# Macaron block on eight cores: an integer weight load moved to another queue, a wait on its stash added, and the second LayerNorm taken in another order

## The chip, the cores and the metric

The kernel runs on one Trainium2 chip, on 8 cores. Each core computes one of the eight batch entries (2048 tokens by 1024 features) with the same program; no core waits for another. The metric is device time in microseconds of the slowest core.

## The reference, cut to what matters

The block is: half a feed-forward step, an attention step, half a feed-forward step, each with a LayerNorm ahead and a residual.

```
def ffn(x):                      # k0 [2048,4096], k1 [4096,4096], k2 [4096,1024], booleans
    W = lambda k: where(k, 1.0, -1.0)
    h = concatenate([x, -x], -1)
    h = relu(s0 * h @ W(k0)) * 2
    h = relu(s1 * h @ W(k1)) * 2
    return s2 * h @ W(k2)

def attn(x):                     # causal linear attention, 16 heads of 64, buckets of 64
    q = softmax(scale * x @ Wq.T per head);  k = elu(scale * x @ Wk.T) + 1;  v = x @ Wv.T
    context = cumsum over buckets of k^T v, divided by (cumsum of sum k + eps), shifted by a bucket
    return (q @ context) @ Wo.T + bo

x = x + 0.5 * ffn(layernorm(x))
x = x + attn(layernorm(x))
x = x + 0.5 * ffn(layernorm(x))
```

Since the input of the first layer is [x, -x], the kernel uses one weight matrix of half the height for it: W(k0[:1024]) - W(k0[1024:]), which is 2 * (k0 upper - k0 lower).

## The kernel before, in words

There is no scheduler. The program appends instructions to five streams (one an engine) in the order in which Python calls `b.op` and `b.dma` (lines 64 to 107), and each instruction carries the semaphore waits of what it reads. A DMA stands in the stream of the engine that issues it, and an engine runs its stream in order: a DMA on ScalarE is issued only after every activation ahead of it. The DMAs of SP, ScalarE (ACT) and GpSimd (POOL) rotate over eight semaphores each (qs, qa, qg), and a DMA also waits for the one eight before it on its own rotation (line 101).

**First feed-forward** (`ffn_phase`). The tokens are taken in two halves of 1024. The first LayerNorm half fills `xnf`. Then `l0_half` (line 402) makes layer 0: eight blocks `nb` of 512 hidden features. In the first half of the first feed-forward only (`build and half == 0`, lines 409 to 430) each block's weights are made from the integers:

- `ta`, a DMA on SP, loads the upper half of k0's block (128 x 8 x 512 bytes, 512 KB) into `u8a`; `tb`, a DMA on ScalarE, loads the lower half into `u8b`. Both wait for the subtraction of the block before, which frees the two buffers.
- L418, VectorE: the subtraction into `wst[:, nb % 2]`; it waits for both loads, for the matmuls of block nb-2 and for the stash of block nb-2 (two weight slots alternate).
- L424, VectorE: the product with the scale, in place.
- `st_["t_w_stash"]`, a DMA on SP: the finished block (1 MB, bf16) is written to `d0_scr` in DRAM, from where later halves read it.
- L446, TensorE: 64 matmuls of 128x128 by 128x512 (4 groups of features by 2 of tokens by 8 deep), which wait for `tslot`, the product. L457, ScalarE: eight Relu evictions into `a1`.

Meanwhile POOL has issued four casting DMAs that turn the attention weights from float32 to bf16 in DRAM (`wprep`, `wbf_scr`); nothing gates them, so they start at the program's start. Layer 1 (L512) and layer 2 (L572) follow, with weight blocks that POOL loads into four slots. During layer 2 of the second half, `ln2_hook` (line 995) computes the statistics of the attention's LayerNorm. For the 128-token chunks gc 0 to 7 it loads them from DRAM, one after the other, into the two pages of `xst` (page gc % 2), so that chunks 6 and 7 are what stands in `xst` at its end. For chunks 8 to 15 it reads them where layer 2 leaves them.

**Attention** (`attn_phase`, line 599). After a fence of all engines and queues, all 16 chunks are loaded from `x_scr`: 0 to 7 by ScalarE's queue into the space of `qfm`, 8 to 15 by POOL's into the space of `kk`; SP issues 16 DMA transposes for Wq and Wk. For each chunk in turn L297 (VectorE) normalizes into `qb`, eight transposes on TensorE (L310) fill `ps_t`, and L317 (VectorE) copies them to `xn2fm`. `ps_t` and the order in VectorE's stream make it a chain, chunk after chunk. Then the projections (L700) run for q, k and v over 16 chunks each.

Of the kernel before, what the change touches and what calls it, by code (L numbers as in the profile page):

```python
# [162 lines left out]
def build_program(debug_phases=("ffn1", "attn", "ffn2")):  # L163
    b = B()
# [13 lines left out]
    x_dram = nc.dram_tensor("x_scr", [T, D], F32, kind="Internal").ap()  # L178
# [11 lines left out]
    xst = b.sb("xst", [128, 2, D], F32)  # L190
    qb = b.sb("qb", [128, 2, D], BF16)
# [14 lines left out]
    def t7_set(i, tok):  # L206
# [5 lines left out]
    st_ = {  # L212
        "pa": [None, None, None],
        "pb": [None, None, None, None],
        "pt": None,
        "xst": [None, None],
        "qb": [None, None, None],
        "qfm_gate": None,
        "scr1": None, "scr2": None,
        "mv": [None, None],  # L220
# [38 lines left out]
    def ln_load(src_ap, gc, page, pg_tok, q):  # L259
        return b.dma(q, page, chunk_ap(src_ap, gc),  # L260
                     reads=(pg_tok, st_["x_load_extra"][gc]))
# [60 lines left out]
    def ffn_phase(src_ap, dst_ap, fstack, l2_hook=None):  # L322
# [5 lines left out]
        u8b = b.sb(None, [128, 8, 512], U8, fstack)  # L328
# [72 lines left out]
        def l0_half(half, t_xn_last):  # L401
            rp = 0
            nonlocal a1_evac
            for nb in range(8):
                sl = nb % 2
                dsl = wst[:, sl, 0:8, :]
                d0blk = d0_dram[:, nb * 512:(nb + 1) * 512].rearrange(
                    "(cc p) n -> p cc n", p=128)
                if build and half == 0:
                    ta = b.dma("sync", u8a[:],  # L410
                               k0_d[0:D, nb * 512:(nb + 1) * 512]
                               .rearrange("(cc p) n -> p cc n", p=128),
                               reads=(u8_tok[0],))
                    tb = b.dma("scalar", u8b[:],
                               k0_d[D:2 * D, nb * 512:(nb + 1) * 512]
                               .rearrange("(cc p) n -> p cc n", p=128),
                               reads=(u8_tok[1],))
                    td1 = b.op("vector", lambda E, ds=dsl: E.tensor_tensor(  # L418
                        out=ds, in0=u8a[:], in1=u8b[:], op=ALU.subtract),
                        (ta, tb, st_["wstq"][sl], st_["slot_stash"][sl], t_d0c),  # L420
                        "dv")
                    u8_tok[0] = td1
                    u8_tok[1] = td1
                    tslot = b.op("vector", lambda E, ds=dsl: E.tensor_scalar(  # L424
                        out=ds, in0=ds, scalar1=deriv[:, 0:1], scalar2=None,
                        op0=ALU.mult), (), "dv")
                    st_["t_w_stash"] = b.dma("sync", d0blk, dsl,
                                             reads=(tslot,))
                    st_["slot_stash"][sl] = st_["t_w_stash"]
                    tslot = (tslot,)  # L430
                else:
                    tslot = b.dma("sync", dsl, d0blk,
                                  reads=(st_["wstq"][sl], st_["slot_stash"][sl],
                                         st_["t_w_stash"]))
                    tslot = (tslot,)
                grp_last = None
                for n in range(4):
                    for th in range(2):
                        rp = st_["rot7"]
                        st_["rot7"] = (rp + 1) % 7  # L440
                        reads = tslot + (t_xn_last[th * 4 + 3], t7_tok(rp))
                        mm = None
                        for cch in range(8):
                            mm = b.op("tensor",
                                      lambda E, r=rp, nn=n, t2=th, c3=cch, ds=dsl:
                                      E.matmul(tile7[r],  # L446
                                               ds[:, c3, nn * 128:(nn + 1) * 128],
                                               xnf[:, c3, t2 * 512:(t2 + 1) * 512],
                                               start=(c3 == 0), stop=(c3 == 7)),
                                      reads if cch == 0 else (),  # L450
                                      "pe" if cch == 7 else None)
                        grp_last = mm
                        ev_reads = [mm]
                        if nb == 0 and n == 0 and th == 0:
                            ev_reads.append(st_["prev_xh_store"])
                        tev = b.op("scalar", lambda E, r=rp, nn=n, t2=th, nb2=nb:
                                   E.activation(out=a1[:, nb2 * 4 + nn,  # L457
                                                       t2 * 512:(t2 + 1) * 512],
                                                in_=tile7[r], func=AF.Relu),
                                   ev_reads, "ac")  # L460
                        t7_set(rp, tev)
                        a1_evac = tev
                st_["wstq"][sl] = grp_last
            l0_pe[half] = grp_last
# [134 lines left out]
    def attn_phase(astack):  # L599
# [23 lines left out]
        def ln2_page(gc):  # L623
            if gc < 8:
                return qfmx[:, gc, :]
            j = gc - 8
            return kkxs[:, 2 * j:2 * j + 2, :, :].rearrange(
                "p a b c -> p (a b c)")

        ln2_tx = [ln_load(x_dram, gc, ln2_page(gc), st_["ln2_stage_gate"],  # L630
                          "scalar" if gc < 8 else "gpsimd")
                  for gc in range(16)]
        stage_tok = [None] * 16
        xn2_tok = [None] * 16
        twt_cur = None
        soft_pe = ("pe", b.cnt["pe"], "_")
        for gc in range(16):
            if gc == 8:
                twt_cur = load_wT(wTsA, 0, (t_wstash["q"],))
            mv, trs = st_["ln2_pre"][gc]  # L640
            sl = gc % 2
            txn, _ = ln_apply(sl, gc, mv, trs, ln2_tx[gc], ln2_page(gc),
                              False, lambda s: qb[:, s, :], (st_["qb"][sl],))
            stage_tok[gc] = txn
            st_["qb"][sl] = txn
            t_xn_last = transpose8(
                lambda c3, s=sl: qb[:, s, c3 * 128:(c3 + 1) * 128],
                xn2fm[:, :, gc * 128:(gc + 1) * 128], (txn, soft_pe))
            st_["qb"][sl] = t_xn_last
            xn2_tok[gc] = t_xn_last  # L650
# [29 lines left out]
        for wname in ("q", "k", "v"):  # L680
# [7 lines left out]
                                    ("pe", b.cnt["pe"], "_")))  # L688
            else:
                wTs, twt = wTsA, twt_next  # L690
            for tc in range(16):
                rb = tc % 3
                mm = None
                for jb in range(2):
                    for c in range(8):
# [10 lines left out]
                if wname == "q":  # L706
# [7 lines left out]
                        axis=AX.X), (t4,), "dv")  # L714
                    b.op("vector", lambda E: E.reciprocal(
                        out=stat[:, 5, :], in_=stat[:, 5, :]), (), "dv")
                    sl = tc % 3
                    t7 = b.op("vector", lambda E, s=sl: E.tensor_tensor(
                        out=qpage(s).rearrange("p (h e) -> p h e", e=64),
                        in0=scr1[:, :].rearrange("p (h e) -> p h e", e=64),  # L720
# [6 lines left out]
                elif wname == "k":  # L727
                    while st_["q_pend"]:
                        q_flush()
                    sl = tc % 2  # L730
                    tmx = b.op("vector", lambda E, r=rb, s=sl: E.tensor_scalar(
                        out=qb[:, s, :], in0=qps[r][:, :], scalar1=SCALE_Q,
                        scalar2=0.0, op0=ALU.mult, op1=ALU.max),
                        (mm, st_["qb"][sl]), "dv")
                    te = b.op("scalar", lambda E, r=rb: E.activation(  # L735
                        out=scr1[:], in_=qps[r][:, :], func=AF.Exp,
                        scale=SCALE_Q), (tmx, st_["scr1"]), "ac")
                    qps_tok[rb] = te
                    t4_reads = (te, tmx, stage_tok[8 + tc // 2])
                    if tc == 15:  # L740
                        t4_reads = t4_reads + (st_["qb"][2],)
                    t4 = b.op("vector", lambda E, t2=tc, s=sl: E.scalar_tensor_tensor(
                        out=kk[:, t2, :, :].rearrange("p h e -> p (h e)"),
                        in0=scr1[:], scalar=1.0, in1=qb[:, s, :],
                        op0=ALU.min, op1=ALU.add), t4_reads, "dv")
                    st_["scr1"] = t4
                    st_["qb"][sl] = t4
                    kk_tok[tc] = t4
                else:
                    tv = b.op("vector", lambda E, t2=tc, r=rb: E.tensor_copy(  # L750
                        out=vv[:, t2, :, 0:128], in_=qps[r][:, :]
                        .rearrange("p (h e) -> p h e", e=128)), (mm,), "dv")
                    qps_tok[rb] = tv
                    vv_tok[tc] = tv
# [332 lines left out]
```

How the kernel before makes its waits and increments, by code:

```python
                def body(E):  # L131
                    seen = {}
                    nw = 0
                    for item in self.streams[eng]:
                        if item[0] == "w":
                            _, s, v = item
                            if seen.get(s, 0) >= v:
                                continue
                            seen[s] = v
                            if nw >= 2:
                                E.nop(nofuse=True)
                                nw = 0
                            E.wait_ge(self.semh[s], v)
                            nw += 1
                        else:
                            nw = 0
                            _, fn, inc, amt = item
                            inst = fn(E)
                            if inc is not None and amt:
                                inst.then_inc(self.semh[inc], amt)
```

## Time and profile before

| what | us |
|---|---|
| median of 2 timed runs (3943.73 to 3957.61) | 3950.67 |
| the profiled execution, its own time | 3531.66 |
| its span, core 3, the slowest | 3530.1 |
| spans of the eight cores | 3495.0 to 3530.1 |
| mean granted TensorE clock of the cores | 0.938 to 0.946 |
| TensorE busy with matmuls, core 3 | 3073.8 |

The profiled execution is one run of the same program; the two timed runs took 419 us longer, and the traces hold nothing of them. All rows below are of core 3 in the profiled execution, and their times count from its first instruction.

### The profile page before, as it was taken

How to read it: one execution, taken by the hardware profiler on the slowest of the kernel's cores; microseconds unless marked ns; L12 is line 12 of the kernel's file. 1: busy time of each engine (PE TensorE's matmuls, PEld its weight loads, DVE VectorE, ACT ScalarE, POOL GpSimd, SP SyncE). 2: the span in 40 equal slices, each digit the busy share in tenths (PEclk: the TensorE clock that was granted, in tenths of full speed). 3: DMA queues.
4: the chain of work that ended last, by engine and by line, in shares of the span. 5: the costliest groups of instructions: out<-in, count | busy, mean ns of one | idle time of the engine just before them, and what ended most of it. 6: DMA issues, size and time to landing. Idle time of an engine off the chain costs nothing.

```text
span 3530.1 us, 35801 instructions; the slowest of 8 cores (3495.0 to 3530.1 us)
## 1 busy us (share of the span) xinstructions
PE 3073.8 (87%) x14600; PEld 1404.2 (40%) x14600; DVE 532.5 (15%) x593; ACT 444.5 (13%) x745; POOL 168.7 (5%) x208
## 2 busy tenths in 40 slices
PE   0558999988999999984886678999999989999998
PEld 0223444443444444432433423444444444444443
DVE  2122111111000000023655831000000000000001
ACT  0111101000120110000112402210110021011000
POOL 0000000000000000000000000000000000000000
PEclk9878999999999999996996588999999999999999
DMA  9225546455232231437101072332233222221322
GB/s 146 78 78 152 171 126 175 135 162 174 84 96 72 71 96 60 133 112 168 22 14 30 12 232 58 91 100 78 84 90 105 84 85 91 75 84 60 96 96 96
DMA packets 223409, 350.48 MB, mean 99 GB/s; under 512 B 40720, under 2 KB 171792, under 8 KB 222992
## 3 DMA queue, kind: packets, MB, share of 16 engines
q0 software_dynamic: 79072, 191.91, 20.2%
q1 hardware_dynamic: 131104, 134.79, 13.0%
q10 hardware_dynamic: 13072, 21.50, 1.9%
q8 instruction: 118, 1.93, 0.2%
q14 instruction: 43, 0.35, 0.0%
HBM read 251.70 MB, written 83.89 MB: 95 GB/s over the span
## 4 chain that ended last, share of the span: by engine, by line
PE 80%; DMA 7%; DVE 7%; ACT 2%; issue 2%; another core or an unknown queue 1%; ACTq 0%; DVEq 0%; SPq 0%; POOL 0%; POOLq 0%
PE ps_b L512 28%; PE ps_a L512 21%; PE ps_b L446 8%; PE ps_b L572 6%; PE ps_a L446 6%; PE ps_a L572 4%; PE ps_b L700 2%; DMA sb<-k2pm_scr 2%; DMA sb<-k 2%; PE ps_b L968 1%; DMA xst<-x_scr 1%; DMA sb<-x_scr 1%; PE ps_t L310 1%; DVE sb L418 1%
## 5 line engine op out<-in xcount | busy, mean ns | idle before, releaser
L512 PE MATMUL ps_b<-sb 128*128 128x512 bf16 x4672 | 1301.6, 380 | 13.0 <-ACT stat L286 5.3
L512 PE MATMUL ps_a<-sb 128*128 128x512 bf16 x3520 | 1052.5, 380 | 11.1 <-ACT stat L289 2.8
L512 PEld LDWEIGHTS ps_b<-sb 128*128 128x128 bf16 x4672 | 457.2, 98 | 565.2 <-issue 22.8
L512 PEld LDWEIGHTS ps_a<-sb 128*128 128x128 bf16 x3520 | 344.7, 98 | 428.4 <-issue 19.7
L446 PE MATMUL ps_b<-sb 128*128 128x512 bf16 x1168 | 271.4, 392 | 98.5 <-DVE sb L424 98.5
L572 PE MATMUL ps_b<-sb 128*128 128x512 bf16 x1216 | 279.5, 391 | 45.3 <-DMA sb<-k2pm_scr 21.4
L446 PE MATMUL ps_a<-sb 128*128 128x512 bf16 x880 | 206.8, 393 | 51.8 <-DVE sb L424 34.3
L523 ACT ACTIVATE sb<-ps_b,deriv 128x512 bf16<-128x512 f32 x146 | 100.3, 687 | 914.8 <-PE ps_b L512 904.5
L446 PEld LDWEIGHTS ps_b<-sb 128*128 128x128 bf16 x1168 | 117.0, 100 | 246.5 <-issue 117.5
L572 PE MATMUL ps_a<-sb 128*128 128x512 bf16 x832 | 188.9, 389 | 17.5 <-DMA sb<-k2pm_scr 10.9
L572 PEld LDWEIGHTS ps_b<-sb 128*128 128x128 bf16 x1216 | 120.7, 100 | 202.1 <-issue 70.2
L310 PE MATMUL ps_t<-idn,qb 128*128 128x128 bf16 x472 | 48.8, 266 | 139.2 <-DVE qb L297 103.0
L523 ACT ACTIVATE sb<-ps_a,deriv 128x512 bf16<-128x512 f32 x110 | 75.6, 687 | 711.1 <-PE ps_a L512 678.6
L100 POOL DMA_DIRECT2D sb<-k1pm_scr x96 | 84.8, 884 | 1604.0 <-PE ps_b L512 595.2
L446 PEld LDWEIGHTS ps_a<-sb 128*128 128x128 bf16 x880 | 88.2, 101 | 164.6 <-issue 67.9
L317 DVE COPY sb<-ps_t 128x1024 bf16<-128x1024 bf16 x64 | 44.3, 692 | 705.2 <-PE ps_t L310 703.8
L580 DVE SCALAR_TENSOR_TENSOR sb<-ps_b,deriv,sb 128x512 f32<-128x512 f32 x38 | 28.5, 751 | 798.8 <-PE ps_b L572 798.4
L700 PE MATMUL ps_b<-sb 128*128 128x512 bf16 x528 | 128.2, 403 | 9.8 <-ACT scr L735 8.9
L572 PEld LDWEIGHTS ps_a<-sb 128*128 128x128 bf16 x832 | 82.4, 100 | 122.7 <-issue 29.6
L457 ACT ACTIVATE sb<-ps_b 128x512 bf16<-128x512 f32 x146 | 87.2, 597 | 287.1 <-PE ps_b L446 287.1
L457 ACT ACTIVATE sb<-ps_a 128x512 bf16<-128x512 f32 x110 | 65.7, 597 | 449.9 <-PE ps_a L446 449.9
L310 PEld LDWEIGHTS ps_t<-idn,qb 128*128 128x128 bf16 x472 | 38.4, 119 | 155.3 <-issue 151.3
(93 smaller groups left out, 1018.0 us busy)
## 6 DMA issues: line engine op xcount, KB each, us to landing
sb<-k1pm_scr POOLq DMA_DIRECT2D x96, 1024.0 KB, 7.0
sb<-k POOLq DMA_DIRECT2D x40, 1024.0 KB, 5.8
k1pm_scr<-sb SPq DMA_DIRECT2D x32, 1024.0 KB, 9.3
sb<-d_scr SPq DMA_DIRECT2D x24, 1024.0 KB, 6.2
sb<-k2pm_scr POOLq DMA_DIRECT2D x24, 1024.0 KB, 8.0
x_scr<-sb SPq DMA_DIRECT2D x21, 512.0 KB, 2.6
sb<-x_in SPq DMA_DIRECT2D x19, 512.0 KB, 10.9
sb<-x_scr SPq DMA_DIRECT2D x19, 512.0 KB, 12.7
```

What stands on the lines that cost most here:

```text
L100: E.dma_start(out=o, in_=i, transpose=tr),
L310: ttr = b.op("tensor", lambda E, c3=c2: E.transpose(ps_t[:, c3, :], src_getter(c3), idn[:]), tuple(reads) + (st_["pt"], t_id), "pe")
L317: tev = b.op("vector", lambda E, d=dst_ap: E.tensor_copy(out=d, in_=ps_t[:, :, :]), (ttr,), "dv")
L418: td1 = b.op("vector", lambda E, ds=dsl: E.tensor_tensor(out=ds, in0=u8a[:], in1=u8b[:], op=ALU.subtract), (ta, tb, st_["wstq"][sl], st_[" ...
L446: E.matmul(tile7[r], ds[:, c3, nn * 128:(nn + 1) * 128], xnf[:, c3, t2 * 512:(t2 + 1) * 512], start=(c3 == 0), stop=(c3 == 7)),
L457: E.activation(out=a1[:, nb2 * 4 + nn, t2 * 512:(t2 + 1) * 512], in_=tile7[r], func=AF.Relu),
L512: E.matmul(tile7[r], wst[:, qq, c3 % 8, nn * 128:(nn + 1) * 128], a1[:, c3, t2 * 512:(t2 + 1) * 512], start=(c3 == 0), stop=(c3 == 31)),
L523: E.activation(out=a2[:, nb2 * 4 + nn, t2 * 512:(t2 + 1) * 512], in_=tile7[r], func=AF.Relu, scale=deriv[:, 1:2]),
L572: E.matmul(tile7[r], a2[:, c3, tt * 128:(tt + 1) * 128], wst[:, qq, c3 % 8, :], start=(c3 == 0), stop=(c3 == 31)),
L580: E.scalar_tensor_tensor(out=xh[:, tt, nb2 * 512:(nb2 + 1) * 512], in0=tile7[r], scalar=deriv[:, 2:3], in1=xh[:, tt, nb2 * 512:(nb2 + 1) * ...
L700: E.matmul(qps[r][:, j2 * 512:(j2 + 1) * 512], xn2fm[:, c3, t2 * 128:(t2 + 1) * 128], w[:, c3, j2 * 512:(j2 + 1) * 512], start=(c3 == 0), ...
L968: E.matmul(ops_[r][:, j2 * 512:(j2 + 1) * 512], at[:, c3, t2 * 128:(t2 + 1) * 128], w[:, c3, j2 * 512:(j2 + 1) * 512], start=False, stop=( ...
```

## The change

It has three parts. In layer 0's building half, `tb` is issued by SP right behind `ta`. The matmuls of a block wait, beside the product L424, for the stash of the block to have landed in DRAM. And the attention's LayerNorm takes its chunks in the order 6, 7, 0 to 5, 8 to 15, with 6 and 7 read from `xst` where the hook left them, so that ScalarE's queue has six page loads in place of eight; the projections run over the chunks in this order too, and the rotation of their buffers goes by the position in it.

```diff
-                    tb = b.dma("scalar", u8b[:],
+                    tb = b.dma("sync", u8b[:],
...
                     st_["slot_stash"][sl] = st_["t_w_stash"]
-                    tslot = (tslot,)
+                    tslot = (tslot, st_["t_w_stash"])
...
+        ln2_order = [6, 7, 0, 1, 2, 3, 4, 5] + list(range(8, 16))
+        ln2_tx = [None if gc in (6, 7) else
+                  ln_load(x_dram, gc, ln2_page(gc), st_["ln2_stage_gate"],
                           "scalar" if gc < 8 else "gpsimd")
                   for gc in range(16)]
...
-        for gc in range(16):
+        for pos, gc in enumerate(ln2_order):
...
+            sl = pos % 2
+            if gc in (6, 7):
+                txn, _ = ln_apply(gc % 2, gc, mv, trs, None, xst[:, gc % 2, :],
+                                  True, lambda s: qb[:, s, :],
+                                  (st_["qb"][sl],))
...
-            for tc in range(16):
-                rb = tc % 3
+            for pos, tc in enumerate(ln2_order):
+                rb = pos % 3
...
-                    sl = tc % 3
+                    sl = pos % 3
...
-                    sl = tc % 2
+                    sl = pos % 2
```

SP's stream at the program's start, before (the first two blocks of layer 0; `sb<-k` is a load of k0, `d_scr<-sb` the stash, qs0 to qs7 SP's rotating semaphores, dv VectorE's):

```order
L100 DMA sb<-x_in 128x1024 x3
L100 DMA sb<-k 128x8x512
L100 DMA d_scr<-sb 128x8x512 [waits dv]
L100 DMA sb<-k 128x8x512
L100 DMA d_scr<-sb 128x8x512 [waits dv]
L100 DMA sb<-k 128x8x512 [waits qs0]
```

and the same place now:

```order
L100 DMA sb<-x_in 128x1024 x3
L100 DMA sb<-k 128x8x512 x2
L100 DMA d_scr<-sb 128x8x512 [waits dv]
L100 DMA sb<-k 128x8x512
L100 DMA sb<-k 128x8x512 [waits qs0]
L100 DMA d_scr<-sb 128x8x512 [waits dv,qs1]
```

Two loads now stand between two stashes. In ScalarE's stream the second load stood behind the eight evictions of the block before:

```order
L457 ACTIVATE sb<-ps_b 128x512 x4
L457 ACTIVATE sb<-ps_a 128x512 x3
L457 ACTIVATE sb<-ps_b 128x512
L100 DMA sb<-k 128x8x512
L457 ACTIVATE sb<-ps_b 128x512 x3
```

and now no load stands between the evictions. TensorE's stream at the start of layer 0, now (before, the first of these rows waits for dv alone, and no NO_OP stands there):

```order
L445 MATMUL ps_b<-sb 128x512 [waits dv,qs6]
L445 MATMUL ps_b<-sb 128x512 x31
L445 MATMUL ps_a<-sb 128x512 x24
L445 MATMUL ps_b<-sb 128x512 [waits ac]
L445 MATMUL ps_b<-sb 128x512 x7
L141 NO_OP [waits dv,qs1]
L445 MATMUL ps_b<-sb 128x512 [waits ac]
```

qs6 and qs1 are the stashes of blocks 0 and 1. VectorE's stream at the start of the attention, the difference in one piece:

```order
-L297 TENSOR_SCALAR qb<-sb,stat 128x1024 [waits dv]
+L297 TENSOR_SCALAR qb<-xst,stat 128x1024 [waits qg7,dv]
+L317 COPY sb<-ps_t 128x8x128 [waits pe,dv]
+L297 TENSOR_SCALAR qb<-xst,stat 128x1024 [waits dv]
+L317 COPY sb<-ps_t 128x8x128 [waits pe,dv]
+L297 TENSOR_SCALAR qb<-sb,stat 128x1024 [waits qa3,dv]
```

Two chunks that wait for no page load stand ahead of the first that does (qa3 is the load of chunk 0; qg7 is part of the fence), and two loads' waits are gone further down.

## Rows read from the trace of the kernel before

**Rows 1.** The page: costliest groups (busy, mean ns, idle before and releaser), layer 0.

```profile
L446 PE MATMUL ps_b<-sb 128*128 128x512 bf16 x1168 | 271.4, 392 | 98.5 <-DVE sb L424 98.5
L446 PE MATMUL ps_a<-sb 128*128 128x512 bf16 x880 | 206.8, 393 | 51.8 <-DVE sb L424 34.3
```

**Rows 2.** Windows, first and last block: length, busy us by engine, clock, DMA.

```profile
102.60:130.50 27.90, 16.78 (x64) 6.84 (x64) 5.71 (x2) 4.78 (x8) 0.00 (x0) 0.85 0.26 76
...
295.30:312.20 16.90, 15.98 (x64) 6.68 (x64) 2.83 (x4) 4.78 (x8) 0.13 (x1) 0.88 0.43 140
```

**Rows 3.** Timeline, loads and stash around block 1: start, duration, instruction, idle before.

```profile
120.22 0.39 ACTq L100 DMA_DIRECT2D sb<-k  x1
124.51 4.42 DVE L418 TENSOR_TENSOR sb<-sb 128x4096 bf16<-128x4096 uint8 x1 [22.04 <-DMA sb<-k]
...
130.40 0.37 SPq L100 DMA_DIRECT2D d_scr<-sb  x1
...
130.87 0.53 SPq L100 DMA_DIRECT2D sb<-k  x1
```

**Rows 4.** DMA issues near block 1 (KB, us to landing): 120.22, 130.40, 130.87.

```profile
sb<-k ACTq DMA_DIRECT2D x1, 512.0 KB, 4.1
...
d_scr<-sb SPq DMA_DIRECT2D x1, 1024.0 KB, 6.7
...
sb<-k SPq DMA_DIRECT2D x1, 512.0 KB, 7.1
```

**Rows 5.** Timeline, the program's start: the loads and the stash of block 0.

```profile
2.91 0.52 SPq L100 DMA_DIRECT2D sb<-k  x1
...
44.75 0.39 ACTq L100 DMA_DIRECT2D sb<-k  x1
...
102.56 0.37 SPq L100 DMA_DIRECT2D d_scr<-sb  x1
```

**Rows 6.** DMA queues, 20 to 88 us: packets, MB, share of 16 engines.

```profile
q0 software_dynamic: 281, 7.64, 99.2%
q1 hardware_dynamic: 283, 0.14, 1.1%
q10 hardware_dynamic: 157, 0.08, 0.4%
```

**Rows 7.** DMA issues of block 0: at 2.91, at 102.56.

```profile
sb<-k SPq DMA_DIRECT2D x1, 512.0 KB, 93.3
...
d_scr<-sb SPq DMA_DIRECT2D x1, 1024.0 KB, 6.3
```

**Rows 8.** Timeline, TensorE in layer 0 of the second half, no gaps.

```profile
1018.10 7.07 PE L446 MATMUL ps_b<-sb 128*128 128x512 bf16 x32
1025.01 5.34 PE L446 MATMUL ps_a<-sb 128*128 128x512 bf16 x24
```

**Rows 9.** Windows: a stretch of the v projection and one of layer 1.

```profile
1834.00:1896.00 62.00, 60.03 (x239) 25.06 (x237) 18.85 (x16) 1.49 (x3) 0.00 (x0) 0.81 0.03 4
...
2300.00:2400.00 100.00, 100.00 (x477) 45.80 (x475) 6.20 (x10) 11.99 (x20) 6.42 (x8) 1.00 0.28 81
```

**Rows 10.** Timeline: page loads; applies of chunks 5, 6, 15; first projection.

```profile
1621.90 4.71 ACTq L100 DMA_DIRECT2D sb<-x_scr  x8
...
1647.72 0.81 DVE L297 TENSOR_SCALAR qb<-sb,stat 128x1024 bf16<-128x1024 f32 x1 [0.97 <-DMA sb<-x_scr]
...
1652.23 0.81 DVE L297 TENSOR_SCALAR qb<-sb,stat 128x1024 bf16<-128x1024 f32 x1 [1.67 <-DMA sb<-x_scr]
...
1678.74 0.81 DVE L297 TENSOR_SCALAR qb<-sb,stat 128x1024 bf16<-128x1024 f32 x1
...
1680.87 9.23 PE L700 MATMUL ps_b<-sb 128*128 128x512 bf16 x32 [0.16 <-issue]
```

**Rows 11.** DMA issues: POOL's loads in 1615 to 1700; the eighth transpose, at 1664.96.

```profile
sb<-x_scr POOLq DMA_DIRECT2D x8, 512.0 KB, 26.6
...
sb<-wbf_scr SPq DMA_TRANSPOSE x1, 6.1
```

More of the change, by code:

```diff
@@ L426, in l0_half @@
                         op0=ALU.mult), (), "dv")
-                    st_["t_w_stash"] = b.dma("sync", d0blk, dsl,
-                                             reads=(tslot,))
+                    st_["t_w_stash"] = b.dma("sync", d0blk, dsl, reads=(tslot,))
                     st_["slot_stash"][sl] = st_["t_w_stash"]
-                    tslot = (tslot,)
+                    tslot = (tslot, st_["t_w_stash"])
                 else:
@@ L628, in ln2_page @@
                 "p a b c -> p (a b c)")
-        ln2_tx = [ln_load(x_dram, gc, ln2_page(gc), st_["ln2_stage_gate"],
+        ln2_order = [6, 7, 0, 1, 2, 3, 4, 5] + list(range(8, 16))
+        ln2_tx = [None if gc in (6, 7) else
+                  ln_load(x_dram, gc, ln2_page(gc), st_["ln2_stage_gate"],
                           "scalar" if gc < 8 else "gpsimd")
@@ L640, in attn_phase @@
             mv, trs = st_["ln2_pre"][gc]
-            sl = gc % 2
-            txn, _ = ln_apply(sl, gc, mv, trs, ln2_tx[gc], ln2_page(gc),
-                              False, lambda s: qb[:, s, :], (st_["qb"][sl],))
+            sl = pos % 2
[3 more added lines that the diff above has]
+                                  (st_["qb"][sl],))
+            else:
+                txn, _ = ln_apply(sl, gc, mv, trs, ln2_tx[gc], ln2_page(gc),
+                                  False, lambda s: qb[:, s, :],
+                                  (st_["qb"][sl],))
             stage_tok[gc] = txn
```

## The prediction
> **What bounds the kernel now.** I read the page first. TensorE holds most of the chain that ended last, so mainly its gaps can be won. The list of groups says where they are: the matmuls of layer 0 (L446) stood idle 98.5 + 34.3 = 132.8 us behind the product L424 [rows 1]. The windows by block show the rhythm: the first lasts 27.9 us though TensorE works 16.8 us in it, and the seven from 102.6 to 295.3 take 192.7 us; the eighth, without a gap behind it, lasts 16.9 us [rows 2]. Seven gaps of 11.1 us are 78 us, and the other 55 us stand ahead of block 0.
>
> The timeline of one block says why [rows 3]. At 120.22, block 0's last eviction done, ScalarE issues the second load of block 1, since the DMA stands behind the evictions in its stream. It lands 4.1 us later [rows 4], and 6.1 us after that the product is made and its stash goes out at 130.40, when TensorE starts too. The other load, on SP, went out with the stash before and was there long ago: the gap is the place of one DMA in ScalarE's order, not a lack of bandwidth.
>
> **The load moves to SP.** Take the issue of a block's stash as the clock tick, since it comes right behind the product. SP issues behind it the two loads of the next block. The first is issued 0.47 us after the stash and lands 7.1 us later, at 7.6 [rows 3, 4]. The second brings another 512 KB in the same queue. What 512 KB more cost there has two nearest rows: the first load lands 0.9 us after the stash (7.6 less 6.7), and a stash of 1 MB takes 2.6 us longer than a lone load of 512 KB (6.7 less 4.1). I take the middle, 1.7, and it lands at 9.3. As the wide ends I keep 0.5 us (its issue alone) and 4.1 us (a whole lone load). From landing to the next stash issue is 130.40 - 124.3 = 6.1 us, of which the subtraction is 4.42 [rows 3]. So a tick is 15.4 us, with 14.2 and 17.8 as ends.
>
> TensorE must not need more. A block is 64 matmuls. In the second half's layer 0, where it never stops, 32 start within 6.91 us (1018.10 to 1025.01) [rows 8], so 64 take 13.8 us. Hence the DMA and VectorE chain sets the pace, and a gap of about 1.6 us stays in each block. The two weight slots allow it: the subtraction of block n+2 needs the end of block n, which comes 6.4 + 0.1 + 13.8 = 20.3 us after the tick of n, and its loads are there only at 15.4 + 9.3 = 24.7 us.
>
> Seven ticks are 107.8 us in place of 192.7: -84.9 us.
>
> **The matmuls wait for the stash.** The stash of block 0, issued at 102.56 [rows 5], landed after 6.3 us [rows 7]; that of block 1 after 6.7 [rows 4]. Block 0 has no cover: TensorE starts 6.3 us later. Blocks 1 to 7 keep the same distance from their ticks, so the wait shifts TensorE once and isn't paid per block; queued behind it are only the block's own matmuls and, through them, the evictions. SP itself doesn't wait for the landing. Cost: +6.3 us, and if stashes landed at once it would be 0; were one to take longer late in the row, its excess counts once.
>
> **Block 0's loads.** The SP load issued at 2.91 landed after 93.3 us, at 96.2, and the ScalarE load went out at 44.75 [rows 5, 7]. They lie among the casts of the attention weights, which keep the 16 DMA engines 99.2% busy from 20 to 88 us [rows 6]. Between 20 and 88 us the casting queue and SP's queue moved 281 and 283 packets, one for one, and ScalarE's 157 from 44.75 on [rows 6]: a 512-byte packet of a load goes through only after a large one of the casts. Behind `ta` in the same queue, `tb` gets no turn of its own, so some 157 of its 1024 packets that went early now go in the rush after the casts. At 1024 packets in 1.7 us that is 0.3 us; I take +0.4. The bounds are -0.3 and +1.7 us (the whole load behind the other).
>
> The Trainium skill (DMA: Bandwidth & Descriptors, section Queues, rings and completion order) says that a DMA engine goes round its queues and drains a packet of some 9 to 17 descriptors at each turn. The one-for-one count of this trace and the landing at 96.2 speak against it, and the sum goes by them; what it would give is rival 5.
>
> **The end of layer 0.** Block 7 began at 295.37 after an 11 us gap, with a granted clock below full for part of it (mean 0.88; 0.85 over block 0 and its gap) [rows 2], and took 16.9 us. After gaps of 1.6 us I expect most of it at full clock, 13.8 us: -3.0 us (bounds -3.1 and 0). The Trainium skill (TensorE: Matmul & The Clock Gate, Part 1) has the clock at 1.2 GHz after idleness and at 2.4 GHz after sustained work, which fits these two windows.
>
> What follows cannot take it back by its order: POOL's loads of k1 wait for blocks 6 and 7 as before, and the first two slots' matmuls of layer 1 wait for them in the same distances. No stretch after it gets other work.
>
> Layer 0: -84.9 + 6.3 + 0.4 - 3.0 = -81.2 us.
>
> **The attention's LayerNorm.** The fence ends near 1621.9, where the loads go out, and VectorE idles until the first has landed. It is fed by landings up to chunk 6 at 1652.23 (1.67 us idle ahead of it), and from there each chunk takes (1678.74 - 1652.23) / 9 = 2.95 us up to the sixteenth [rows 10]. Now chunks 6 and 7 fill the time from 1622 to 1628, before VectorE runs into the landings again: those of the chunks up to 5 aren't hastened by loads that are missing behind them, and chunk 5 starts at 1647.7 as before [rows 10]. Then eight chunks of POOL's (8 to 15) follow at 2.95 each, the last at 1671.3: -7.4 us. POOL's loads must be there: with a median of 26.6 us to landing [rows 11] half are in by about 1652, in the order of need. The first projection also needs eight transposed pieces of Wq; the eighth, issued at 1664.96, landed 6.1 us later at 1671.1 [rows 11], 2.4 us ahead of the projections' new start at 1680.87 - 7.4 = 1673.5 [rows 10]. The bounds are 0 (other transfers take over) and -9. The projections' new order changes no count.
>
> **Sum.** -81.2 - 7.4 = -88.6 us. The profiled execution would go from 3531.7 to 3443.1 us. The two timed runs had a median of 3950.67, 419 us above it, without any trace. I take the same difference off: 3862 us. The difference is from fixed transfers, two VectorE instructions and an order of issue, and none of them scales with whatever made those runs longer, unless it is TensorE's clock, which is the first rival.
>
> **Rivals.**
>
> 1. *The clock pays for it.* In 1834 to 1896, in a dense stretch of a projection, the granted clock was 0.81 on this core; in layer 1 with TensorE busy throughout it was 1.00 [rows 9]. If layer 0, once dense, runs at 0.81 and the gapped one didn't, a matmul takes 0.216 / 0.81 = 0.267 us, a block 17.1 us, and TensorE sets the pace: seven blocks 119.6, so -73.1 + 6.7 + 0 - 7.4 = -74 us: 3877. For it: the timed runs were longer by an eighth, which slower matmuls would explain. Against it: 100 us at 1.00. The Trainium skill (TensorE: Matmul & The Clock Gate, Part 1) advises to budget 1.95 GHz, 0.81 of 2.4, when all cores run dense matmuls; by that every block is 17.1 us. This trace agrees in one stretch of 62 us and disagrees in the long ones.
>
> 2. *The loads are the bound, more than I think.* The second load lands a whole lone load behind the first, tick 17.8: seven are 124.6, so -68.1 + 6.7 - 3.0 - 7.4 = -72 us: 3879. For it: eight cores now all ask for 2 MB in one burst. Against it: the 0.9 us of the first load behind a stash twice its size.
>
> 3. *Slower: the stash and the two loads queue.* In the attention's LayerNorm POOL's 512 KB loads took 26.6 us with other queues in flight [rows 11]. If stash and loads, now one burst in one queue, landed only 26.6 us after the tick, a tick would be 32.7 us, and the sum +36 + 6.7 - 3.0 - 7.4 = +32 us: 3983. It decides from 7 x tick = 192.7 + 3.7 us on, a tick of 28.1, a landing 22.0 us after the tick. Against it: the DMA engines are busy 0.26 of block 0's window [rows 2], and the casts are over by then.
>
> 4. *It does little.* The timed runs may be longer for a reason that swallows the gaps (layer 0 bound by something the profiled run doesn't show). Then only part is seen: about 3920.
>
> 5. *Both loads get through beside the casts.* If SP's queue passed them by, the product would be made long before the casts end, and only its stash would wait for that end, near 96 us. TensorE would start at some 97 in place of 109.3: -101 us, 3850. Against it: one packet for one [rows 6]. This is what the page's turns of 9 to 17 would bring about.
>
> **How the numbers follow.** Chances: the forecast 0.60, rival 1 0.17, rival 2 0.10, rival 3 0.04, rival 4 0.07, rival 5 0.02. About 2%, 79 us here, is what a measurement of this kernel can tell from no change. The forecast's 88.6 lies only 10 us beyond it, and the two timed runs are 14 us apart: I give it 5 in 6 to come out beyond, 0.50; rival 5 adds 0.02, and rivals 1 and 2 lie 5 to 7 us inside and may cross it, 0.05 together. So faster 0.57, within 0.39, slower 0.04. The range: below, a tick of 14.2 (-8.4), clock or LayerNorm a little better and 5 us of scatter, 3845. Above, rivals 1 and 2 with LayerNorm's gain lost and scatter, and a part of rival 4: 3915.
>
> **What would show it.** In the new profile: blocks of layer 0 start 15.4 us apart, with a gap of 1 to 2 us ahead of each that ends with the stash; the first begins near 109.3; layer 1 begins near 231; no DMA on ScalarE between the Relus; clock near 1.00 in blocks 2 to 7. VectorE's sixteenth LayerNorm apply stands 49.4 us after the loads' issue, where it stood 56.8. It is wrong if the starts are 17 us apart at a clock of 0.81 (rival 1), if the subtraction waits longer than 9.5 us after a stash issue (rival 2, 3), or if block 0 begins far from 109.

## The result and the profile after

The changed kernel is faster. In the comparison its median is 3444.13 us of 11 runs (3431.59 to 3854.93), beside 3675.79 us of 10 runs of the kernel before (3514.29 to 4081.09), and the ratio of undisturbed runs is 0.9766, with a 95% interval of 0.9747 to 0.9785. In some executions of either kernel the cores of one die or of both show a lower mean granted clock (0.80 to 0.93; in one of the kernel before, of 3950.34 us, 0.825 to 0.829) and the whole takes 1 to 16% longer; by their times both timed runs shown ahead of the prediction (3950.67) were such, and the ratio leaves these executions out.

The profiled execution took 3433.78 us. The mean span of its eight cores went from 3514.4 to 3423.0 us, -91.4, at a clock of 0.953 to 0.955 (0.938 to 0.946 before). The slowest core is now core 2, at 3432.2. Its page, the costliest groups of layer 0 (busy, mean ns, idle before and its releaser), answers to [rows 1]:

```profile
L445 PE MATMUL ps_b<-sb 128*128 128x512 bf16 x1168 | 262.4, 383 | 64.0 <-DMA d_scr<-sb 63.0
L445 PE MATMUL ps_a<-sb 128*128 128x512 bf16 x880 | 200.4, 384 | 20.9 <-DMA sb<-d_scr 16.0
```

The idle time fell from 98.5 + 51.8 to 64.0 + 20.9 us. What ends most of it is no longer the product but the stash (`d_scr<-sb`), the wait that the change added; the 16.0 us of the second row (`sb<-d_scr`) are reloads of the stashed blocks in later halves. Of the 63.0, 61.0 are the one stretch ahead of block 0, and only the last 6.9 us of that stretch come after the stash's issue. From block 1 on the waits for a stash are some 7 us in all on this core.

The timeline of core 3, blocks 0 to 2, answers to [rows 3, 5]: start, duration, instruction, idle before it.

```profile
102.62 0.37 SPq L100 DMA_DIRECT2D d_scr<-sb  x1
103.03 2.03 SPq L100 DMA_DIRECT2D sb<-k  x2
...
109.31 8.78 PE L445 MATMUL ps_b<-sb 128*128 128x512 bf16 x32 [59.72 <-DMA d_scr<-sb]
...
112.08 4.43 DVE L418 TENSOR_TENSOR sb<-sb 128x4096 bf16<-128x4096 uint8 x1 [9.54 <-DMA sb<-k]
...
118.04 0.37 SPq L100 DMA_DIRECT2D d_scr<-sb  x1
...
127.65 4.42 DVE L418 TENSOR_TENSOR sb<-sb 128x4096 bf16<-128x4096 uint8 x1 [9.75 <-DMA sb<-k]
...
133.61 0.37 SPq L100 DMA_DIRECT2D d_scr<-sb  x1
```

Both loads now go out with the stash. The tick is, as in the prediction, the issue of a block's stash. The subtraction starts 9.5 us after the tick of block 0 and 9.6 after the next (127.65 - 118.04), and the ticks are 15.4 and 15.6 us apart. The loads ended the wait, as forecast. The windows of the same core, one block each (columns as in [rows 2]):

```profile
109.30:124.80 15.50, 15.49 (x64) 6.61 (x65) 5.71 (x2) 4.18 (x7) 0.00 (x0) 1.00 0.51 135
124.80:140.20 15.40, 14.01 (x65) 6.21 (x65) 5.71 (x2) 5.38 (x9) 0.00 (x0) 1.00 0.50 135
...
216.70:231.60 14.90, 13.99 (x65) 6.20 (x66) 2.82 (x4) 5.45 (x10) 1.10 (x2) 1.00 0.49 141
```

TensorE works 14.0 us in a block of 15.4, at a granted clock of 1.00 (2.4 GHz). The last window stands where [rows 2] had 16.90 us at 0.88.

The attention's LayerNorm differs by core. On core 3 the timeline of VectorE reads (answering to [rows 10]; `xst` holds chunks 6 and 7):

```profile
1543.44 0.81 DVE L297 TENSOR_SCALAR qb<-xst,stat 128x1024 bf16<-128x1024 f32 x1 [2.42 <-issue]
...
1559.10 0.81 DVE L297 TENSOR_SCALAR qb<-sb,stat 128x1024 bf16<-128x1024 f32 x1 [3.88 <-DMA sb<-x_scr]
...
1592.73 0.81 DVE L297 TENSOR_SCALAR qb<-sb,stat 128x1024 bf16<-128x1024 f32 x1
```

On core 2, the slowest, one chunk waited much longer for its page:

```profile
1536.51 0.81 DVE L297 TENSOR_SCALAR qb<-xst,stat 128x1024 bf16<-128x1024 f32 x1 [2.41 <-issue]
...
1558.59 0.81 DVE L297 TENSOR_SCALAR qb<-sb,stat 128x1024 bf16<-128x1024 f32 x1 [13.24 <-DMA sb<-x_scr]
...
1593.92 0.81 DVE L297 TENSOR_SCALAR qb<-sb,stat 128x1024 bf16<-128x1024 f32 x1
```

From the first apply to the sixteenth that is 49.3 us on core 3 and 57.4 on core 2.

To find where the time went I marked the start of every stage in each core's trace, and took means over the eight cores of one profiled execution. "Step" is the mean distance of two stashes' issues; "LN" is from the issue of the page loads to the first projection.

| kernel | block 0 starts | block 0 to layer 1 | step | LN, mean (least to most) | span |
|---|---|---|---|---|---|
| before | 104.1 | 209.3 | 27.49 | 60.9 (54.3 to 70.2) | 3514.4 |
| changed | 110.5 | 122.0 | 15.53 | 51.8 (46.4 to 59.3) | 3423.0 |
| difference | +6.4 | -87.3 | | -9.1 | -91.4 |

The sum of the three is -90.0 us. The rest of the 91.4 is spread over the other stages: the q, k and v projections are 1.8 us shorter, the others moved by some 1 us or less, up and down.

### The profile page after: what moved, and what is told of

The parts are those of the page before. It is cut to its first block, busy times and chain, and to the rows that moved or that the text cites. A ratio compares the mean times of both kernels' runs of the same rounds, so it can differ in the third digit from the quotient of the medians.

```text
span 3432.2 us, 35800 instructions; the slowest of 8 cores (3413.3 to 3432.2 us)
## 1 busy us (share of the span) xinstructions
PE 3042.7 (89%) x14600; PEld 1397.5 (41%) x14600; DVE 532.5 (16%) x593; ACT 444.5 (13%) x745; POOL 169.2 (5%) x208
## 4 chain that ended last, share of the span: by engine, by line
PE 79%; DMA 8%; DVE 7%; ACT 2%; issue 2%; another core or an unknown queue 1%; DVEq 0%; SPq 0%; ACTq 0%; POOL 0%; POOLq 0%
PE ps_b L511 29%; PE ps_a L511 22%; PE ps_b L571 6%; PE ps_b L445 6%; PE ps_a L445 5%; PE ps_a L571 4%; DMA sb<-k 2%; DMA sb<-k2pm_scr 2%; PE ps_b L707 2%; PE ps_t L310 1%; PE ps_b L975 1%; DMA xst<-x_scr 1%; DMA sb<-x_scr 1%; ACT sb L819 1%
## 5 line engine op out<-in xcount | busy, mean ns | idle before, releaser
L511 PEld LDWEIGHTS ps_a<-sb 128*128 128x128 bf16 x3520 | 344.3, 98 | 425.7 <-issue 15.8
L445 PE MATMUL ps_a<-sb 128*128 128x512 bf16 x880 | 200.4, 384 | 20.9 <-DMA sb<-d_scr 16.0
## 6 DMA issues: line engine op xcount, KB each, us to landing
k1pm_scr<-sb SPq DMA_DIRECT2D x32, 1024.0 KB, 10.3
```

The costliest lines, as they stand in the source:

```text
L445: E.matmul(tile7[r], ds[:, c3, nn * 128:(nn + 1) * 128], xnf[:, c3, t2 * 512:(t2 + 1) * 512], start=(c3 == 0), stop=(c3 == 7)),
L511: E.matmul(tile7[r], wst[:, qq, c3 % 8, nn * 128:(nn + 1) * 128], a1[:, c3, t2 * 512:(t2 + 1) * 512], start=(c3 == 0), stop=(c3 == 31)),
```

## The experiments

Ten runs were made on three chips, each beside executions of the kernel before on the same chip. The ratios of the wait alone, the changed kernel again, the late casts and both edits to the loop rest on two executions each. My theory was that of the prediction; its rivals were that the stash wait itself is paid in each block, that the saving is of the loads' bandwidth and not of their place, and that the LayerNorm's gain is scatter.

### The changed kernel without the stash wait, run twice

```
-                    tslot = (tslot, st_["t_w_stash"])
+                    tslot = (tslot,)
```

> The changed kernel without the wait of layer 0's matmuls for the stash. My theory (the wait shifts TensorE once, because the tick of about 15.5 us is set by stash, two loads, subtraction and product, and not by TensorE): block 0 starts some 6.5 us earlier, near 103 to 105 us, the blocks are still 15.5 us apart, layer 1 starts near 226 instead of 232.6 (mean of the cores), and the whole is 6 to 7 us shorter than the changed kernel: ratio to the kernel before 0.972. Rival (the wait is paid in every block): the blocks come 14 us apart or less and the whole is 15 to 50 us shorter, ratio 0.96 to 0.97. Rival (the wait costs nothing): layer 1 starts near 232, ratio 0.9766.

> The changed kernel without the wait, a second time. My theory now: without the wait TensorE starts each block 6.5 us earlier, which puts the 16 KB packet of the instruction queue (one in every second block) at 6.6 us behind the stash's issue, into the middle of the loads; the DMA engine that carries it holds 1/16 of the loads back for 1.0 to 1.7 us, and those blocks are 16.2 to 16.9 us long, the others 15.5. Beyond that, two cores of a pair whose bursts fall together load at 42 ns a packet in place of 30, and their blocks are 17 to 18 us long. Expected: mean distance 15.9 to 16.6 us, the alternation of 15.5 and 16.7 on most cores, layer 1 starts 0 to 5 us earlier or later than in the changed kernel of this chip, whole within 4 us of it. Rival (the first run was a chance): blocks 15.5 us apart on all cores and the whole 6.5 us shorter than the changed kernel.

Measured: 0.9766 [0.9745, 0.9787], and on a second chip 0.9764 [0.9745, 0.9783]. The changed kernel, on that same second chip, gave 0.9788:

> The changed kernel itself, on the chip on which the kernel without the wait runs next. The first run without the wait had blocks 16.5 us apart in the mean of the cores (15.7 to 17.9), on another chip than the changed kernel with its 15.5. If the wait is what keeps the blocks at 15.5, they are 15.4 to 15.7 us apart on every core here, and the ratio is 0.975 to 0.978. If it was the chip, they are 16 us and more apart here too.

with an interval of 0.9729 to 0.9846. So taking the wait away wins nothing that can be measured. The traces show why: there is a gain and a loss. From the last tick to layer 1 it takes 20.1 us in both executions with the wait and 15.6 in both without, so the wait costs 4.5 us there. It costs more at block 0, 6.8 and 7.4 us from the tick, but the last stash, with no loads behind it, lands in 4.9 us.

Against that gain, the steps are 16.47 and 16.35 us without the wait, where the two runs with it have 15.53 and 15.90: +6.6 and +3.1 us over seven steps. The first tick was 2.3 us later in the first run without the wait than in the first with it, by chance as far as the traces tell, and equal in the second two. Together layer 1 starts 4.3 us later and 1.4 us earlier than with the wait. I had expected unchanged steps without the wait, and steps of 15.4 to 15.7 us on every core of the changed kernel's repetition (they were 15.5 to 16.4), and missed both.

What lengthens them was sought in the single packets of the queues. Two things coincide with long steps.

First, the instruction queue. On core 3 of the first run the steps are 16.5, 15.6, 16.6, 15.4, 16.7, 15.4 and 16.9 us. These are the queues of a long block (136.6 to 146.9) and of a short one (121.1 to 130.4): packets, MB, share of 16 engines, and the loads' median us to landing.

```profile
q1 hardware_dynamic: 3120, 2.10, 74.9%
q8 instruction: 1, 0.02, 0.6%
...
sb<-k SPq DMA_DIRECT2D x2, 512.0 KB, 8.2
```

```profile
q1 hardware_dynamic: 3120, 2.10, 83.8%
...
sb<-k SPq DMA_DIRECT2D x2, 512.0 KB, 7.8
```

The same 3120 packets move; the long block has one 16 KB packet of instructions besides, which holds one DMA engine for 1.0 to 1.2 us, and its second load lands 10.3 us after the tick in place of 9.2. Over the eight cores, the 9 steps in which it starts 6.3 to 7.9 us after the stash's issue, amid the loads, are 16.2 to 16.9 us long; on cores 4 and 7 the 6 in which it starts at 8.3 or later are 15.5 or 15.6. In the changed kernel all 32 such packets start at 7.9 or later, and their steps are 15.1 to 15.9. That the packet comes later there because the wait holds TensorE some 6 us behind the tick is my reading; no kernel moved the packet alone. The second run has no such packet between 3 and 8 us, so the alternation was not what I had expected of it. But outside its pair of cores in step (the next point) the 17 steps in which the packet starts 0.9 to 2.4 us after the tick are 16.2 us long in the mean (15.7 to 17.0), and the other 25 are 15.8.

Second, pairs of neighbouring cores in step. In the first run cores 0 and 1 issue their first stash at 106.4 and 106.1, in the second run cores 2 and 3 at 105.5 and 105.4, and all seven steps of these four cores are long (16.9 to 18.4), with a load's packet taking 32 to 45 ns in the mean of a step where core 3 of the first run has 30. With the wait such pairs exist too: cores 4 to 7 of the repeated changed kernel begin with steps of 17.0 to 17.9 us at 105.0 to 105.4, but come down to 15.3 to 15.6 by the fifth. Why that dissolves with the wait and not without was not settled. Leaving these pairs out, the mean steps are 16.0 and 15.9 us without the wait and 15.5 and 15.6 with it, so 0.3 to 0.5 us a step remain of the difference.

### The wait alone, in the kernel before

```
-                    tslot = (tslot,)
+                    tslot = (tslot, st_["t_w_stash"])
```

> The kernel before with the wait for the stash alone, the second load still behind the evictions on ScalarE. My theory: here TensorE is part of the loop (the load is issued behind its last eviction), so the same wait is paid in each of eight blocks: 6.3 to 6.7 us each, blocks 34 us apart, +50 us, ratio 1.014. Rival (a stash wait always shifts TensorE once): +6.5 us, ratio 1.002. The same edit worth 6.5 us in one kernel and 50 us in the other would show that what decides is whether TensorE stands in the loop.

Measured: 1.0146 [1.0116, 1.0175], some 51 us, or 6.4 for each of eight blocks. The mean steps of cores 2 to 5 are 34.2 to 34.6 us, 6.7 to 7.1 more than 27.49; the other four have 34.9 to 37.2. This profiled execution took 3761.27 us, where the two behind the ratio took 3575.27 and 3576.93, so the ratio is the better witness. The timeline of core 3, SP's stashes of blocks 0 to 2:

```profile
105.23 0.37 SPq L100 DMA_DIRECT2D d_scr<-sb  x1
...
139.85 0.37 SPq L100 DMA_DIRECT2D d_scr<-sb  x1
...
174.01 0.37 SPq L100 DMA_DIRECT2D d_scr<-sb  x1
```

Here the next load is issued behind the evictions, hence behind the matmuls, hence behind the wait: more than 6 us come back in every block. With both loads on SP nothing that ends last in the tick passes through TensorE, and the same wait is paid once. Its price depends on whether the waiting engine is in the loop.

### The LayerNorm's order alone

The changed kernel with `tb` back on ScalarE and without the wait.

> The kernel before with the LayerNorm's order and the two pages from xst alone; layer 0 as before. My theory: from the issue of the page loads to the first projection 51 to 53 us in the mean of the cores, where it was 60.8 (7 to 10 us shorter), two steps of 2.95 us and the end of a wait; the whole -7 to -10 us, ratio 0.9975. Rival (the slow landings shift with it and take it back, as on the slowest core of the changed kernel, which took 59.3): -0 to -3 us, ratio 0.999 to 1.000.

Measured: 0.998 [0.9968, 0.9991]; LN takes 53.5 us (47.8 to 59.7) in place of 60.9, -7.4. The order is worth its 7 us, though the stage scatters by 10 us and more between cores. The other executions bear it out: with the old order the means over the cores are 60.9 and 60.7 us, with the new one and ungated transposes they are 50.9 to 56.7 in eight executions, 53.5 in their mean.

This run also isolates the move of the load. It and the kernel without the stash wait differ by `tb`'s queue alone: block 0 to layer 1 takes 208.6 us here and 130.7 there, and the ratios are 0.998 and 0.9766.

### The page loads without the transposes

In the changed kernel SP's eight transposes of Wq, and behind them in its stream the eight of Wk, wait for the last page load of ScalarE's queue.

```
-                twt_cur = load_wT(wTsA, 0, (t_wstash["q"],))
+                twt_cur = load_wT(wTsA, 0, (t_wstash["q"], ln2_tx[5]))
```

> The changed kernel with SP's transposes of Wq (and all behind them) held back until the page of chunk 5 has landed. In the changed kernel the fourth or fifth apply waits 3 to 13 us for a page (from the loads' issue to the first projection 46 to 59 us by core, mean 51.8). If the transposes in flight are what delays that page, the wait goes, and the projections start 49 to 50 us after the loads' issue on every core, unless the eighth transpose is then the last to arrive (16 pieces at 1.2 to 2.6 us each, the eighth some 12 to 16 us behind its gate, near 35 to 40 us). Whole: -2 us in the mean, -5 on the slowest core, ratio 0.976. If the loads are slow by themselves, nothing changes; if the transposes become late, the projections start after 55 us.

Measured: 0.9738 [0.9721, 0.9755], and LN takes 46.3 to 47.6 us on every core. SP's queue and the only apply of core 0 that still waits (cores 3 and 7 have two such waits each, of 0.2 to 0.6 us):

```profile
1565.02 25.58 SPq L100 DMA_TRANSPOSE sb<-wbf_scr  x16
...
1565.12 0.81 DVE L297 TENSOR_SCALAR qb<-sb,stat 128x1024 bf16<-128x1024 f32 x1 [0.49 <-DMA sb<-x_scr]
```

In the changed kernel, on core 2, the transposes go out among the page loads:

```profile
1537.06 57.42 SPq L100 DMA_TRANSPOSE sb<-wbf_scr  x16
```

Core 2 lost 13.24 us to one page there. Its 16 transposes are issued over 57.4 us, and over 25.6 us when gated. Gated, nothing of note is left beside the chain of chunks: fifteen distances of 2.95 us between the applies and 2.0 us from the last apply to the first projection are 46.2 us. Both the stage's length above that and its scatter came from the transposes in flight.

### The casts moved away from the start

The casts of the attention weights are issued in 16 parts during layer 1 of the second half; the rest is the changed kernel.

```
-                st_["wprep_fn"]()
-                st_["wprep_fn"] = None
...
+                    if build and half == 1 and q % 2 == 1:
+                        st_["wprep_fn"](nb * 2 + q // 2)
```

> The changed kernel, stash wait kept, with the casts of the attention weights taken from the program's start into layer 1 of the second half, in 16 pieces behind every second weight load of POOL. My theory (block 0 waits for its loads only because they lie among the casts): both loads have landed by 25 us, block 0's subtraction starts when VectorE is done with the LayerNorm, near 50, TensorE starts near 62 instead of 110, the blocks stay 15.5 us apart, and the whole is 45 to 50 us shorter than the changed kernel: ratio 0.963, less what the casts cost in layer 1 (0 to 10 us). Rival (the loads are slow for another reason, such as their 512-byte packets): block 0 still starts after 90 us and the ratio stays near 0.977. Rival (the casts cost in layer 1 what they gave): TensorE waits for k1pm loads there, 20 us and more.

Measured: 0.9623 [0.9595, 0.9651]; block 0 starts at 64.5 in place of 110.5, the rest stands (step 15.83). The first loads landed at 22.5 and 24.0 us on core 2, before the LayerNorm was done (its subtraction starts at 51.7), so the wait ahead of block 0 was the casts'. On core 2 of the changed kernel, 20 to 88 us (answering to [rows 6]):

```profile
q0 software_dynamic: 272, 7.34, 96.2%
q1 hardware_dynamic: 272, 0.14, 1.5%
```

One packet for one again, a 512-byte packet of a load behind each large one of the casts.

### Taking the stash out of the loop, in two ways

The loop of a step is stash, two loads, subtraction, product. If its 15.4 us are that, either of two edits should leave TensorE as the bound. (a) No wait, and the next block's loads issued behind the subtraction, ahead of the product and its stash. (b) No wait, casts late, and a second pair of pages for the integers, so that loads are issued a block ahead.

```
(a) +                    if nb < 7:
    +                        ld8(nb + 1)      # between L418 and L424
(b) +                    for nx in ([0, 1] if nb == 0 else [nb + 1] if nb < 7 else []):
    +                        xa, xb = u8p[nx % 2]
```

> The changed kernel without the wait, with one change of order: SP issues the two loads of the next block right behind the subtraction, ahead of the stash, into the same single pages. My theory (the 15.5 us are stash, loads, subtraction, product, one behind the other; the stash ahead of the loads in the queue costs some 3 us of it, and the product 1.3): the loads land about 6 us behind the subtraction, the loop is some 10.6 us, and TensorE sets the pace with 13.8 us a block. Layer 1 starts 96.7 + 16 us after block 0, near 219 with block 0 at 105 to 106, where it was 235 to 237; 15 us less than without the wait, ratio 0.9725. If the queue's order doesn't matter (the DMA engines interleave the three), the blocks stay 15.5 us or more apart and the ratio 0.9765.

> The kernel with the late casts, without the stash wait, and with a second pair of pages for the integer loads (in the third weight slot, idle in this stage), so that the loads of a block go out ahead of the stash of the block before. If stash and two loads in one burst are what sets 15.5 us a block, the loads now leave the loop, TensorE sets the pace with 13.8 to 14.1 us a block, TensorE starts near 57 us, layer 1 near 170 (188 with the late casts alone), and the whole is 16 to 19 us shorter than with the late casts: ratio 0.957. If VectorE or the slots set the pace, the blocks stay 15.5 us apart and only the wait's 6 us are won: ratio 0.961.

Measured: (a) 0.971 [0.969, 0.9729], block 0 to layer 1 in 113.5 us; (b) 0.9587 [0.9564, 0.961], the same stage in 113.7. Steps settle at 13.8 in both, TensorE's own time for 64 matmuls [rows 8]. In (a), core 3, the loads are issued ahead of the stash, and from the third subtraction on it is TensorE that it waits for:

```profile
102.43 0.99 SPq L100 DMA_DIRECT2D sb<-k  x2
...
103.88 0.52 SPq L100 DMA_DIRECT2D d_scr<-sb  x1
...
108.60 4.43 DVE L421 TENSOR_TENSOR sb<-sb 128x4096 bf16<-128x4096 uint8 x1 [4.86 <-DMA sb<-k]
...
133.33 4.43 DVE L421 TENSOR_TENSOR sb<-sb 128x4096 bf16<-128x4096 uint8 x1 [7.99 <-PE ps_b L450]
```

VectorE in (b), core 4, shows the same releaser:

```profile
73.05 4.43 DVE L429 TENSOR_TENSOR sb<-sb 128x4096 bf16<-128x4096 uint8 x1 [10.26 <-PE ps_b L457]
...
86.87 4.42 DVE L429 TENSOR_TENSOR sb<-sb 128x4096 bf16<-128x4096 uint8 x1 [8.00 <-PE ps_b L457]
```

The subtraction waits for matmuls to free its slot, and no longer for a load. The order of issue (a) does as much for the loop as the second pages of (b).

### All of it together

Casts late, two pages, no stash wait, and the gated transposes.

> The version meant to beat both: late casts, two pairs of integer pages, no stash wait, and SP's transposes held back until chunk 5's page has landed. Each part is additive in my account: 3365 us in the mean of the cores for the first three, less the gate's part of the LayerNorm stage (56.7 us from the loads' issue to the first projection there, 46.6 with the gate): 3355 us in the mean, ratio 0.955 to 0.956. If the parts overlap, 0.958.

Measured: 0.9555 [0.9539, 0.9571], median 3365.32 us of 6 runs, spans 3347.3 to 3362.6 with a mean of 3355.6. It beats both kernels: block 0 at 57.2, 113.6 us to layer 1, LN 46.4 (46.2 to 46.8). Version (b) above, which differs by the gate alone, had an LN of 56.7 (49.9 to 59.8): the second pair of runs that shows what the transposes cost.

## Why the prediction was right or wrong, point by point

**The sum was right, the level it was put on wrong.** The sum gave 3531.7 - 88.6 = 3443.1 us, a ratio of 0.975; measured were 0.9766, and 3433.78 us in the profiled execution. The forecast time of 3862 us, with its range of 3845 to 3915, does not hold the measured median of 3444.13. The step that failed is the last of the sum: "The two timed runs had a median of 3950.67, 419 us above it, without any trace. I take the same difference off: 3862". I carried the 419 us over as if they were the kernel's. They were not: the comparison of the kernel before holds the two timed runs among its ten executions, and five others of the same program took 3514 to 3528 us. As far as the executions with a record of the clock tell, what sets such a time apart is TensorE's clock (3950.34 us at 0.825 to 0.829), the one case that the prediction set aside with "unless it is TensorE's clock". The range should have reached down to the profiled execution's level. That the 88.6 us come off unchanged was forecast as well; for the 3862 it would be a ratio of 0.9776, but the measured ratio leaves out the executions at the lower clock, so it does not show that the same difference comes off there.

**The tick: right.** Forecast 15.4; 15.53 by the mean over cores (15.4 to 15.7 on core 3), and the subtraction 9.5 and 9.6 us behind the first two ticks, where the second load was to land at 9.3. The middle of my two ends, +1.7 us for the second 512 KB, was close; the eight cores' bursts cost nothing more, except for pairs in step.

**The stash wait: right in kind, and in size at block 0.** Forecast +6.3 us once; TensorE starts 6.7 us after the tick on core 3 (109.31 - 102.62), and block 0 by 6.4 us later in the mean. Block 7 starts 5.3 us after its tick on this core (216.72 - 211.46), since the last stash lands in 4.9 us. The kernel with the wait alone shows the other side, more than 6 us in each block. What the prediction did not see is that the wait's removal costs elsewhere: without it the steps are about 0.5 to 0.9 us longer, seven of them, and the net price is nil.

**Block 0's loads: right, by two small errors that cancel.** Core 3 starts block 0 at 109.31, forecast 109.3. The forecast has +0.4 us for the loads and 6.3 for the stash; measured are 0.0 (its first tick stands at 102.62 in both kernels) and 6.7, so the exact hit is luck, by a few tenths. The Trainium skill (DMA: Bandwidth & Descriptors, section Queues, rings and completion order) would have 9 to 17 descriptors go at each turn of a queue. The counts of 272 to 272 disagree, as before: they are 17 of each for each of the 16 DMA engines in 68 us, and the two kinds alternate over the whole window. Rival 5 is refuted, since block 0 did not start at 97.

**The end of layer 0: right in the sum, not in its parts.** Core 3 begins layer 1 at 231.6, forecast near 231, at a clock of 1.00. Block 7 took 14.9 us and not the forecast 13.8. TensorE worked 14.0 us in it at full clock (the last of the three windows above), and 0.9 us are a wait of layer 1's first matmul for the last eviction, which the prediction left out:

```profile
231.58 0.81 PE L511 MATMUL ps_b<-sb 128*128 128x512 bf16 x3 [0.89 <-ACT sb L456]
```

The shorter wait for the last stash took about as much off again: from the last tick to layer 1 the forecast adds 6.3 - 3.0 = 3.3 us, and measured are 20.1 - 16.9 = 3.2. Layer 0 as a whole: -80.7 us on core 3 (312.3 to 231.6), -80.9 in the mean, forecast -81.2.

**LayerNorm: right on the core that I read, a little small in the mean, and absent on the slowest.** Core 3 went from 59.0 to 51.3, -7.7, forecast -7.4, the sixteenth apply 49.2 us behind the loads' issue (forecast 49.4). The mean is -9.1 and scatters, and by the eight executions above some 7 of it are the order's; core 2, the slowest of the new execution, took 59.3 us, 5.0 more than in the kernel before. The assumption that "those of the chunks up to 5 aren't hastened by loads that are missing behind them" says nothing of the transposes, which turned out to be what delays these loads. Gated, the same order takes 46.6 us in the mean.

**The rivals.** Rival 1, the clock: the windows of layer 0 stand at 1.00 in place of the 0.81 it needed. The Trainium skill (TensorE: Matmul & The Clock Gate, Part 1) advises to budget 1.95 GHz for dense matmuls on all cores, and this trace disagrees for these 120 us. Rival 2, a tick of 17.8: only pairs of cores in step came to it, for some blocks of later runs. Rival 3, slower: it needed a landing 22.0 us after the tick; the subtraction started at about 9.5. Rival 4, little: the gain was whole.

**What stays open.** Why a pair's overlap dissolves with the wait and persists without it, and whether the instruction packet makes the long steps or only goes with them.

## What to carry to other kernels

Ask of an added wait whether the waiting engine stands in the loop that sets the pace: if the next transfer is issued from that engine's stream, or behind it, the wait is paid in each turn, and otherwise once. A load that is issued behind evictions is late by its place, not by bandwidth, and issuing it one instruction earlier, ahead of a large store, can win as much as a second buffer. And when timed runs lie far from the profiled execution of the same kernel, predict the ratio and let the range hold both levels.

## What the runs showed that I had not expected

- One 16 KB packet of the instruction queue amid a burst of 2 MB goes with a step that is 0.6 to 1.3 us longer (16.2 to 16.9 against 15.6). It holds one of 16 DMA engines for 1.0 to 1.2 us; that the burst ends with that engine is argued, not shown.
- Two neighbouring cores whose bursts coincide take 17 to 18 us a block in place of 15.5, at 32 to 45 ns a packet of 512 bytes in place of 30.
- DMA transposes in flight delay plain loads of other queues: LN takes 46.4 to 59.3 us with them and 46.3 to 47.6 with the transposes held back, and in the last two versions 49.9 to 59.8 and 46.2 to 46.8.
- Beside casting transfers the first load of 512 KB takes 93 us to land [rows 7], one small packet for each large one; with the casts moved away block 0 starts 46 us earlier.
